# Softmax denominators summed in SBUF by VectorE, with one f32 ones-matmul per head, in an eight-core attention and gated FFN layer

## The reference

```python
xn = layernorm(x)
q  = (xn @ Wq) split into 32 heads of 128        # one shared k and v head of 128
k, v = halves of xn @ Wkv
scores = q k^T * 128**-0.5 + slope[h] * (pos_k - pos_q)      # ALiBi, causal
s = (softmax(scores) @ v) @ Wo
w = qweight * scales + scaled_zeros               # 4096 x 4096, groups of 128
g = silu(xn @ w^T + bias)
out = x + s * g
```

## Time and profile before

| | us |
|---|---|
| median of the runs | 8713.2 (two runs: 8649.6 and 8776.8) |
| the profiled execution | 8538.0 |
| its span on the slowest core | 8536.3 |
| spans of the eight cores | 8497.3 to 8536.3 |
| PE busy over the span | 4815.4 (56%) |
| DVE busy | 1570.2 (18%) |
| ACT busy | 1836.3 (22%) |

### The profile page before, as it was taken

How to read it: one execution, slowest core, us unless ns; L and a number is a source line. 1 busy time by engine, 2 the same in 40 slices (tenths; PEclk the granted TensorE clock), 3 DMA queues, 4 the chain that set the end, 5 groups by cost and what they waited for, 6 DMA issues and landing times.

```text
span 8536.3 us, 52132 instructions; the slowest of 8 cores (8497.3 to 8536.3 us)
## 1 busy us (share of the span) xinstructions
PE 4815.4 (56%) x19057; PEld 1849.8 (22%) x19424; DVE 1570.2 (18%) x1827; ACT 1836.3 (22%) x2712; POOL 0.2 (0%) x4
## 2 busy tenths in 40 slices
PE   0001233337759932106757799687686688987850
PEld 0000001113324422101211244233121122433320
DVE  4441000001110034323232200001312311000012
ACT  6772000000000034203424300001354353000000
POOL 0000000000000000000000000000000000000000
PEclk9999975568879955557878899898788889998975
DMA  7775344477774367990000133543000001335468
GB/s 268 295 295 162 86 101 108 108 147 154 152 154 100 94 177 211 267 326 0 0 24 1 29 87 82 115 100 87 0 0 24 0 0 35 87 86 109 103 159 290
DMA packets 1750777, 987.09 MB, mean 116 GB/s; under 512 B 1529090, under 2 KB 1684738, under 8 KB 1717506
## 3 DMA queue, kind: packets, MB, share of 16 engines
q1 hardware_dynamic: 1242626, 648.17, 30.1%
q10 hardware_dynamic: 507904, 335.58, 13.1%
HBM read 581.01 MB, written 251.66 MB: 98 GB/s over the span
## 4 chain that ended last, share of the span: by engine, by line
PE 52%; DMA 24%; DVE 13%; ACT 5%; issue 3%; SPq 2%; ACTq 0%; DVEq 0%
PE pbE L780 11%; PE pbE L732 10%; PE pqC L451 8%; DMA xntB<-xnh 8%; PE pbE L637 5%; PE pbE L656 5%; DVE rd_f L697 5%; PE pbE L632 5%; PE pbigB L371 4%; DMA wqrC<-wq 4%; DMA xA<-xkv 3%; DMA wobh<-wobD 3%; ACT wfoD L515 2%; DMA xcF<-xq 2%; DVE stA L295 2%
## 5 line engine op out<-in xcount | busy, mean ns | idle before, releaser
L371 PE MATMUL pbigB<-xntB,wkv_bf 128*128 128x512 bf16 x753 | 340.2, 619 | 1413.7 <-DMA xntB<-xnh 1411.2
L451 PE MATMUL pqC<-xntqC,wqbC 128*128 128x512 bf16 x4014 | 939.0, 395 | 330.8 <-DVE wqbC L432 268.6
L780 PE MATMUL pbE<-attnTE,wftslE 128*128 128x512 bf16 x4014 | 903.0, 383 | 218.4 <-DMA wftslE<-wfth 117.4
L681 ACT ACTIVATE ppb<-pbE,bslE 128x512 bf16<-128x512 f32 x1264 | 796.5, 684 | 843.7 <-PE pbE L656 684.8
L732 PE MATMUL pbE<-attnTE,woslE 128*128 128x512 bf16 x4014 | 893.8, 380 | 104.2 <-DVE stslE L737 80.1
L697 DVE RECIPROCAL rd_f<-pbE 1x512 f32<-1x512 f32 x128 | 427.6, 3340 | 1513.1 <-PE pbE L637 1474.4
L637 PE MATMUL pbE<-ppb,c_onec 128*1 128x512 bf16 x1528 | 597.7, 391 | 12.6 <-ACT ppb L681 6.0
L632 PE MATMUL pbE<-ppb,vt 128*128 128x512 bf16 x1475 | 597.0, 405 | 10.2 <-DVE attnTE L713 9.8
L451 PEld LDWEIGHTS pqC<-xntqC,wqbC 128*128 128x128 bf16 x4096 | 411.6, 101 | 858.6 <-issue 414.9
L656 PE MATMUL pbE<-qtsE,kt 128*128 128x512 bf16 x1478 | 558.6, 434 | 63.1 <-DMA tsbE<-tstk 59.0
L780 PEld LDWEIGHTS pbE<-attnTE,wftslE 128*128 128x128 bf16 x4096 | 399.4, 99 | 722.1 <-issue 274.5
(11 more groups left out here) (45 smaller groups left out, 1928.7 us busy)
## 6 DMA issues: line engine op xcount, KB each, us to landing
xA<-xkv SPq DMA_DIRECT2D x48, 2048.0 KB, 10.7
xnh<-xnA ACTq DMA_DIRECT2D x64, 1024.0 KB, 10.9
wqrC<-wq SPq DMA_DIRECT2D x32, 2048.0 KB, 19.4
qwD<-qw SPq DMA_DIRECT2D x32, 2048.0 KB, 9.6
worD<-wo SPq DMA_DIRECT2D x32, 2048.0 KB, 14.6
woslE<-wobh SPq DMA_DIRECT2D x64, 1024.0 KB, 8.9
wftslE<-wfth SPq DMA_DIRECT2D x64, 1024.0 KB, 10.2
xA<-xq SPq DMA_DIRECT2D x16, 2048.0 KB, 12.4
```

Source lines behind the costliest of these rows:

```text
L371: mm_done = P.emit("tensor", lambda e, jj=j, p_=pb, c_=ch, wo_=wofs: e.matmul(pbig[:, 512 * c_:512 * (c_ + 1)], wkv_bf[:, 256 * jj + wo_:2 ...
L451: mm_done = P.emit("tensor", lambda e, jj=j, c_=ch, p_=pb: e.matmul(pq[:, 2048 * p_ + 512 * c_:2048 * p_ + 512 * (c_ + 1)], wqb[p_][:, 128 ...
L681: ex = P.emit("scalar", lambda e, b_=sb, pi=ppi, f_=fi, j_=j: e.activation(ppb[:, 512 * pi:512 * (pi + 1)], pb_[b_][:], AF.Exp, bias=bsl[: ...
L780: mmf = P.emit("tensor", lambda e, g_=gg, qq=q_, p_=pbu, b_=buf, c_=coff: e.matmul(pb_[2 + qq][:], wftsl[p_][:, 128 * g_:128 * (g_ + 1)], ...
```

## The change

The denominator matmul of every step goes. In its place DVE adds the `ppb` tile into an f32 accumulator in SBUF, `accA` (128 x 512 for each head of the pair); for a head's first tile it copies instead. The exponential that later overwrites the `ppb` tile now waits for the value matmul and for this DVE operation. At the end of the pair one matmul per head, f32 on both sides, multiplies an f32 column of ones (`c_onecf`, loaded by one more DMA at the start) with `accA` and gives the 1 x 512 sums that the reciprocal reads. The two `rs_f` tiles become one. The core of the diff:

```diff
+    onescolf = din("onescolf", [128, 1], F32)
+    c_onecf = E(nc.sbuf_tensor("c_onecf", [128, 1], F32))
+    accA = E(nc.sbuf_tensor("accA", [128, 2 * 512], F32))
-    rs_f = [E(nc.sbuf_tensor(f"rs_f{i}", [128, 512], F32)) for i in range(2)]
+    rs_f0 = E(nc.sbuf_tensor("rs_f0", [128, 512], F32))
+    rs_f = [rs_f0, rs_f0]
...
-                            dmm = P.emit("tensor", lambda e, pi=ppi_p, i_=i_p,
-                                         st_=st_p, sp_=sp_p: e.matmul(
-                                pb_[6 + i_][0:1, :], c_onec[:, 0:1],
-                                ppb[:, 512 * pi:512 * (pi + 1)], start=st_, stop=sp_),
-                                waits=[bank_free[6 + i_p]], incs=[("t", 1)])
+                            if st_p:
+                                ac = P.emit("vector", lambda e, pi=ppi_p, i_=i_p: e.tensor_copy(
+                                    out=accA[:, 512 * i_:512 * (i_ + 1)],
+                                    in_=ppb[:, 512 * pi:512 * (pi + 1)]),
+                                    waits=[("s", ex_p), acc_guard[i_p]], incs=[("v", 1)])
+                            else:
+                                ac = P.emit("vector", lambda e, pi=ppi_p, i_=i_p: e.tensor_tensor(
+                                    out=accA[:, 512 * i_:512 * (i_ + 1)],
+                                    in0=accA[:, 512 * i_:512 * (i_ + 1)],
+                                    in1=ppb[:, 512 * pi:512 * (pi + 1)], op=ALU.add),
+                                    waits=[("s", ex_p), last_ac[i_p]], incs=[("v", 1)])
+                            last_ac[i_p] = ("v", ac)
                             last_av[i_p] = av
-                            last_dmm[i_p] = dmm
-                            pp_free[ppi_p] = [("t", dmm)]
+                            pp_free[ppi_p] = [("t", av), ("v", ac)]
...
                         h = heads[i]
+                        dmm = P.emit("tensor", lambda e, i_=i: e.matmul(
+                            pb_[6 + i_][0:1, :], c_onecf[:], accA[:, 512 * i_:512 * (i_ + 1)],
+                            start=True, stop=True),
+                            waits=[last_ac[i], bank_free[6 + i]], incs=[("t", 1)])
+                        acc_guard[i] = ("t", dmm)
                         rc = P.emit("vector", lambda e, i_=i: e.reciprocal(
                             out=rd_f[i_][:], in_=pb_[6 + i_][0:1, :]),
-                            waits=[("t", last_dmm[i]), ("v", rcb_guard[i])], incs=[("v", 1)])
+                            waits=[("t", dmm), ("v", rcb_guard[i])], incs=[("v", 1)])
...
-                            waits=[("t", rmm), ("v", prev_mul)], incs=[("v", 1)])
+                            waits=[("t", rmm), ("v", prev_mul), ("v", mul_guard[0])],
+                            incs=[("v", 1)])
```

More of the change, by code:

```diff
@@ L270, in build_nc @@
                          (c_sz, sz), (c_fb, fb), (c_simh, simh),
-                         (c_onec, onescol), (c_oner, onesrow)):
+                         (c_onec, onescol), (c_oner, onesrow),
+                         (c_onecf, onescolf)):
             P.emit("sync", lambda e, d=dst, s_=src: e.dma_start(out=d[:], in_=s_),
@@ L595, in build_nc @@
             rcb_guard = [0, 0]
+            mul_guard = [0]
+            acc_guard = [("t", 0), ("t", 0)]
             rmm_guard = 0
@@ L625, in build_nc @@
                     last_av = [0, 0]
-                    last_dmm = [0, 0]
+                    last_ac = [("v", 0), ("v", 0)]
                     pend = []
@@ L717, in build_nc @@
                         prev_mul = mul
+                        mul_guard[0] = mul
                         bank_free[4 + i] = ("v", mul)
@@ L874 @@
             onescol=np.ones((128, 1), np.float32).astype(bfdt),
+            onescolf=np.ones((128, 1), np.float32),
             onesrow=np.ones((1, 128), np.float32).astype(bfdt)))
```

## The result

| | before | after |
|---|---|---|
| the profiled execution, us | 8538.0 | 8215.3 |
| its span on the slowest core, us | 8536.3 | 8213.7 |
| attention, both slots, us | 2287.1 | 1939.8 |
| median of all runs, us | 8577.6 (ten runs, 8531.4 to 8776.8) | 8459.3 (eleven runs, 8194.7 to 8605.5) |
| ratio (95%) | | 0.958 (0.952 to 0.964) |

A forecast was written before the change was run, and what follows sets the result against it. PE's issue bounds steps inside a pair, DVE's two reciprocals the gap between pairs. Steps save 420 us, pair ends give back 94: 326 less, 8212 us profiled, 8387 us median, range 8290 to 8640.

The forecast's parts named there:

- the last of the sum: Whole program: the runs' median keeps lying 175 us above the profiled execution, so 8212 us becomes 8387 us.
- The plain step: Attention's unmasked step: falls from 1.69 to 1.27 us, saving 192 us over 457 steps.
- The masked step: Attention's step on the diagonal: falls from 2.12 to 1.33 us, saving 228 us over 288 steps.
- rival E: PE's value matmuls keep 0.31 us, masked steps take 1.48: 43 us less saving, 8430 us; within the forecast's 0.68.
- Who sets the plain step: Unmasked attention steps: ACT sets them at 1.26 us, with DVE at 1.22 and PE at 0.86 (1.05) beneath.
- The pair's extra: Start, slow clock and end of each head pair: 3.0 us instead of 1.5, 94 us back over 64 pairs.
- the slow start: Start of each pair: PE at low clock for some 4 us, costing 1.0 to 1.9 us, 1.1 taken.
- The second f32 matmul: Pair's end, second head: 0.63 us, hidden behind DVE's copy and multiply up to a price of 1.6 us.
- the sign: Between pairs: first reciprocal to next first score stays 10.6 us; 11.0 would speak for a dearer f32 matmul.
- B: Attention steps: DVE bounds, adds start 0.79 us apart, steps 1.58 us; only 112 us less, 8601 us; chance 0.13.
- C: Plain steps: PE's clock falls, each takes 1.67 us; only 143 us less, 8570 us; chance 0.12.
- D: After pair ends: clock stays low in most pairs, steps 1.67 and 2.5 us; 194 us more, 8907 us; chance 0.05.

The follow-up runs named there:

- the first form: The kernel with 128 columns of ones in the final matmul, its reciprocal moved to ACT as exp(-ln(sum)), without the 2^40 factor: attention 1290.5 us, ratio 0.881.

## Why the prediction was right and wrong

**The saving was right; the absolute time was not.** The profiled execution was to be 8212 us and was 8215.3, in part by luck, as the terms below show. The median was to be 8387 us and was 8459.3: in the range, but 72 us above the forecast, and only 118 us below ten runs of the kernel before, where 326 us less had been forecast. The step that failed is the last of the sum: "The median of the runs, 8713, lies 175 us above the profiled one, and I keep that distance". Ten runs of the kernel before put its median at 8577.6, 40 us above the profiled execution, and the kernel after has it 244 us above. The distance is no property of the kernel: it moved by 204 us between two kernels whose profiled executions came out as forecast, and two runs said little of it. The ratio, 0.958 (0.952 to 0.964), holds the forecast ratio 8212 / 8538 = 0.962. The forecast should have been put as a ratio, and its absolute time left at the profiled execution, with a range upward.

**The plain step** was priced 1.27 us and is 1.17 on average: 25 steps of the long pair take 6764.42 - 6735.15 = 29.27 us (its first masked and its fourth score group in PE's timeline). I read ACT's merged row, 1.26 us for two, as the time that two exponentials need. It is 0.58 us from start to start and then 0.68 us, the duration of the second; the mean of 684 ns in the earlier trace rows was there to say so. In a stream only the distance between starts counts, which I had applied to DVE's adds and forgot for ACT. That forecast 192 us for plain steps, where 457 x 0.52 = 238 us came.

**The masked step** was priced 1.33 us and is 1.30: 288 x 0.82 = 236 us, against 228. It is PE's, six matmuls at 0.215 us; the value matmuls run 0.21 us apart when both are ready, so rival E fell.

**Who sets the plain step** was half right. I had ACT at 1.26 us and DVE beneath it at 1.22. The rows have it the other way round, ACT at 1.16 and DVE at 1.20. DVE's price was right, but the order rested on ACT's, so the claim that the wait for the add of two steps before "is covered by 1 us" fails late in a long pair: DVE falls 0.04 us behind at every step until the cover is used up, and the last four plain steps of a 28-step pair and the last eight of a 32-step one are DVE's, 1.20 us. Without the adds they are 1.16. For the time it hardly matters, 0.01 us a step on average.

**The pair's extra** was priced 3.0 us instead of 1.5. By the rows it is 3.1 us in a short pair (3884.55 - 3874.92 = 9.63 us from first score to reciprocal, less 5 x 1.30) and 3.2 in a long one (6772.35 - 6731.18 = 41.17, less 28 x 1.17 and 4 x 1.30). The size is right to 0.2 us, though the first f32 matmul alone costs 1.02 us where I took 0.63 and, in a long pair, first waits 0.42 us for the last add, which I had hidden under the value matmul; so the other terms came out smaller. One of them is the slow start, for which I took some 4 us at the low clock: in the short pair PE's rows go from 0.63 to 0.38 us 2.9 us after the first score (3877.84), in two long ones the low level lasts 3.5 us (6731.18 to 6734.69) and 6.0 (6783.37 to 6789.40). No run splits the extra into its terms.

**The second f32 matmul** was said to be hidden "up to a price of 1.6 us". The bound held and the price was above it: 1.86 us, so that 0.40 us a pair came out, 26 us in all; the run with both final matmuls first gave 23.6 back. Here the forecast named the sign by which it would be seen, 11.0 us from reciprocal to score, and 11.02 it is. The Trainium skill's four passes, "FP8 and Floating Point Precision", section "TensorE Precision Notes", had given estimates of 1.0 and 1.9 us; the trace agrees with 1.02 and 1.86. The bound from the nearest bf16 row was the worse guide, because a row of another operand type carries nothing of what the type costs.

**The sum again:** 238 + 236 = 474 us from the steps; given back 64 x (1.7 + 0.4) = 134 us; 340 us less, beside 347 measured. The forecast of 326 was close by luck: 54 us too little from the steps stood against 40 us too little given back.

**The rivals.** B fell for this kernel, and its price was right: adds chained by hand gave steps of 1.59 us, where B said 1.58, and cost 225 us, where B lay 326 - 112 = 214 us above the forecast. C and D fell: at plain steps 1.16 us apart the granted clock is 1.00, though PE's four matmuls fill only 4 x 0.21 = 0.84 us of that. The swing of the clock that the Trainium skill reports of a kernel with short idles between its groups of matmuls, "TensorE: Matmul & The Clock Gate", section "A second HAM failure mode: psum-queue depth-cycling", did not come here, by that row. PE does fall to the low level at the end of every pair, as before the change.

## What to carry to other kernels

Matmuls with one column of ones cost PE more than full ones: such a matmul started 0.31 us after the one before it, and the next 0.31 us after it, where two full ones are 0.21 apart. Taking one out therefore gave not 0.31 but 0.41 us where PE sets the step (masked: 2.12 to 1.30 us for two). A per-step reduction moved to an idle VectorE was nearly free here as long as its adds did not depend on the one just before (two accumulators in turn: 0.60 us apart, one chain: 0.80). An engine that is 0.04 us a step slower than the one that sets the step is hidden only until the buffers between them are used up, here after some twenty steps. Forecast a stream by the distance between starts and not by a merged row's length, and the whole as a ratio. When the steps have been cut, look at the ends again: the change took 347 us off attention and then the last 13.8 idle us of each pair, on which it had not worked, gave most of 646 us more.

## What the runs showed of the hardware that was not expected

- A matmul of 128 x 512 f32 with f32 weights is two records, together 1.02 us at full clock and 1.86 us at the low one, where bf16 takes 0.38 and 0.58 us.
- DVE's reciprocal of 512 columns takes 3.35 us on one partition as on 128, so spreading the sums ahead of it costs DVE nothing and saves the cast, the matmul and the copy behind it.
- ACT's logarithm and exponential of 128 x 512 take 0.60 and 0.63 us, together less than half of DVE's reciprocal. Sums down to e^-54 are the likely cause of the wrong outputs of the first form; with a factor of 2^40 in the ones the outputs were right, at the same time.
- The add that a wait was put down to (0.42 us, in the run with adds beside the denominators) was not what held ACT: the same 0.43 us stood there without it.
